# Second attention of a two-layer graph network: rough pair, scores, products in TensorE's step

## The reference

```
adj = jnp.maximum(adjacency_matrix, eye)
q, k, v = jnp.einsum('nd,hdk->hnk', node_matrix, Wqs), ...
scores = jnp.einsum('hqk,hmk->hqm', q, k) * kd ** (-0.5)
scores = scores + IDENTITY_BIAS * eye - MASK_VAL * (1.0 - adj)
att = jax.nn.softmax(scores, axis=-1)
return jnp.einsum('hqm,hmk,hko->qo', att, v, Wo)
```

## Time and profile before

| | |
|---|---|
| median of 3 runs | 4923.34 us (4919.93 to 4924.79) |
| the profiled execution's own time | 4912.91 us |
| its span | 4911.1 us |
| PE, DVE, ACT, POOL busy, share of the span | 84%, 74%, 74%, 7% |
| max passes (L1186) | 1024, mean 1224 ns |
| exponentials (L1149), seeds (L1135) | 1024 each, mean 1014 and 1028 ns |
| splits (L1211) | 1024, mean 693 ns |
| scores matmuls (L1081, L1086) | 2048 each, mean 381 and 380 ns |
| copies of `acc` (L1112) | 64, mean 800 ns |

### The profile page before, as it was taken

One profiled execution on the slowest core, in us unless ns is written; L12 is line 12 of the kernel. 1 busy time (PEld: TensorE's weight loads), 2 busy tenths in 40 slices (PEclk: granted clock), 3 DMA queues, 4 the chain that ended last, 5 costly groups with the idle time before them and its releaser, 6 DMA issues. The chain is left out here.

```text
span 4911.1 us, 106706 instructions
## 1 busy us (share of the span) xinstructions
PE 4141.8 (84%) x42500; PEld 2752.0 (56%) x42500; DVE 3639.4 (74%) x6026; ACT 3633.0 (74%) x4642; POOL 343.8 (7%) x527
## 2 busy tenths in 40 slices
PE   7922239889988999699929999999999999999977
PEld 4412228888888888544405555555555555555543
DVE  2245559999999999722238888888888888888834
ACT  1133349999999999511119999999999999999952
POOL 0000000000000000000020211111020202111000
PEclk9955559999999999899959999999999999999999
DMA  1299994544454445445463544545453635445223
GB/s 64 87 303 365 361 342 146 168 161 153 146 166 166 154 139 168 111 144 161 122 168 78 139 119 126 135 105 144 101 155 94 167 86 138 120 122 135 69 74 144
DMA packets 413633, 742.27 MB, mean 151 GB/s; under 512 B 90041, under 2 KB 282745, under 8 KB 376185
## 3 DMA queue, kind: packets, MB, share of 16 engines
q1 hardware_dynamic: 349296, 643.60, 43.5%
q0 software_dynamic: 20608, 75.51, 4.6%
q10 hardware_dynamic: 43280, 16.92, 1.3%
HBM read 567.42 MB, written 168.49 MB: 150 GB/s over the span
## 5 line engine op out<-in xcount | busy, mean ns | idle before, releaser
L1186 DVE CUSTOM_DVE_ANT_0 m_junk<-m_rough,m_rows 128x1024 bf16<-128x1024 f32 x1024 | 1253.4, 1224 | 293.8 <-PE m_rough L1053 226.3
L671 PE MATMUL g_acc<-g_vals,g_pos 128*128 128x130 f16 (+1 forms) x8192 | 1199.0, 250 | 130.9 <-DVE g_neg L626 104.4
L552 ACT ACTIVATE g_step<-g_arow,g_steep 128x512 bf16<-128x512 f32 x2048 | 1258.3, 712 | 58.6 <-DVE g_neg L626 38.2
L1135 ACT ACTIVATE m_scores<-m_strip 128x1024 f32<-128x1024 bf16 x1024 | 1052.9, 1028 | 103.3 <-POOL m_strip L984 39.3
L1149 ACT ACTIVATE m_whole<-m_scores 128x1024 int32<-128x1024 f32 x1024 | 1038.0, 1014 | 34.5 <-PE m_scores L1086 23.6
L1067 PE MATMUL m_acc<-m_v,m_halves 128*128 128x129 f16 (+1 forms) x16384 | 896.8, 208 | 45.3 <-ACT m_got L1112 45.3
L671 PEld LDWEIGHTS g_acc<-g_vals,g_pos 128*128 128x128 bf16 x8192 | 810.7, 99 | 208.5 <-DVE g_neg L626 106.5
L1067 PEld LDWEIGHTS m_acc<-m_v,m_halves 128*128 128x128 f16 x16384 | 750.7, 98 | 280.0 <-issue 185.9
L1081 PE MATMUL m_scores<-m_qA,m_kA 128*128 128x512 f16 x2048 | 780.5, 381 | 5.5 <-ACT m_scores L1135 5.4
L1086 PE MATMUL m_scores<-m_qB,m_kB 65*128 65x512 f16 x2048 | 779.2, 380 | 0.0
L624 DVE TENSOR_TENSOR g_pos<-g_step,g_strip 128x1024 bf16<-128x1024 bf16 x1024 | 679.9, 686 | 87.5 <-ACT g_step L552 65.7
(11 more groups left out here) (146 smaller groups left out, 3158.6 us busy)
## 6 DMA issues: line engine op xcount, KB each, us to landing
g_vals<-scr_gat_v SPq DMA_DIRECT2D x128, 1040.0 KB, 5.3
m_v<-scr_v SPq DMA_DIRECT2D x64, 1032.0 KB, 7.6
b_stage<-in_adj SPq DMA_DIRECT2D x64, 1024.0 KB, 9.8
m_kA<-scr_k_hi SPq DMA_DIRECT2D x128, 512.0 KB, 6.2
scr_row_mask<-b_rowm SPq DMA_DIRECT2D x64, 512.0 KB, 8.8
scr_no_edge_T<-b_colm SPq DMA_DIRECT2D x64, 512.0 KB, 8.3
g_strip<-scr_no_edge_T SPq DMA_DIRECT2D x64, 512.0 KB, 6.8
m_kB<-scr_k_lo SPq DMA_DIRECT2D x64, 512.0 KB, 5.4
```

What stands on the lines that cost most here:

```text
L552: ins = nc.scalar.activation(step[:, j % RING, t, :], arow[:, b, :], ACT.Sigmoid, scale=STEEP, bias=steep[:, b, 2 * j + t:2 * j + t + 1])
L671: mm = pe.matmul(acc[:, b, it, lo:hi], edges, vals[:, b, 2 * j + t, lo:hi], start=j == 0 and t == 0 and lo == 0, stop=j == PAIRS - 1 and t ...
L1135: nc.scalar.activation(scores[:, n % 2], strip[:, 2 * st:2 * st + 2, :].rearrange("p t i -> p (t i)"), ACT.Copy, scale=-BIG / 2).then_inc( ...
L1186: nc.vector.tensor_tensor_reduce(out=junk[:, n % 2], in0=rough[:].rearrange("p a m -> p (a m)"), in1=rows[:, n % TC, n // TC * WIDE:(n // ...
```

## The change

In TensorE's stream alone, the rough pair now stands ahead of the scores of its step, and no longer between scores and products:

```diff
             for g in range(U * STEPS):
-                score(g // STEPS, g // STEPS % SLOTS, g % STEPS)
                 if g + EARLY < U * TILES:
                     max_tile(g + EARLY)
+                score(g // STEPS, g // STEPS % SLOTS, g % STEPS)
                 if g >= LAG:
                     products((g - LAG) // STEPS, (g - LAG) // STEPS % SLOTS, (g - LAG) % STEPS)
```

## The result

The changed kernel takes 5089.46 us (median of 4 runs, 5088.25 to 5094.13) against 4922.35 us (4 runs, 4919.93 to 4924.79): ratio 1.0341, 95% interval 1.0323 to 1.0359, 167 us slower.

What follows compares the result with a forecast made beforehand. A closed chain of waits across ScalarE, VectorE and TensorE, 4.49 us over two steps, becomes the bound: 37.11 us per unit against 33.72, 62.25 x 3.39 = 211 us, plus 2 at the start, gives 5136 us, range 5090 to 5175.

Steps and rivals of the forecast that it cites:

- The chain: Exponential, split, max pass, rough pair, scores, exponential: 4.49 us over two steps, 2.245 per step; before, 5.19 over three.
- split start to max pass start: VectorE link from a split's start to the next max pass's start, put at 0.74 us.
- The other links: Exponential to split 1.04, max pass to rough pair 1.29, rough pair to scores 0.34, scores to exponential 1.08 us.
- The extras: Copy, reduction, division and small matmuls, work done once per unit that lengthens single steps.
- The division: VectorE, round 8: makes split to max pass 1.15 us, adding 0.41, felt by step 9.
- The reduction: VectorE, round 4, over the maxima: makes split to max pass 0.98 us, adding 0.24, felt by step 5.
- Products to rough pair: TensorE behind the copy: 0.70 us, within 5.14 from the exponential of step 2 to that of step 4.
- the odd chain: Odd steps from step 3 at 2.77 through seven links of 4.49; decides the unit's 37.11 us, the even steps giving 36.79.
- The step of TensorE: Cost of the rough pair's new neighbours on TensorE: put at nothing, bounded at 0.1 us per step either way.
- Extras are swallowed: Rival: copy, reduction and division hide in slack between even and odd steps; 36.14 us per unit, 5076 us; 7%.
- The clock: Granted clock stays 1.00; rival: TensorE's falls behind each unit's copy, 5248 us, 3%; harsher form near 6000, 1%.
- The own range: Range of the main forecast alone, 5105 to 5165 us, counting 0.03 us in each chain link as 15 us.

Runs made afterwards that it cites:

- rps: Kernel before, with the order rough pair, products, scores on TensorE, the rough pair ahead of its step's scores: 5582.82 us, ratio 1.1358.
- rsp_maxfirst: Changed kernel with VectorE's max pass ahead of the split in each round: 4941.94 us, ratio 1.0053 to the kernel before.
- rsp_maxfirst_copyearly: Changed kernel with VectorE's max pass ahead of the split and ScalarE's copy of acc ahead of the seed: 4875.44 us, ratio 0.9918 to the kernel before.
- rsp_divlate: Changed kernel with VectorE's division behind the max pass of its round instead of ahead of it: 5065.32 us, ratio 1.0307 to the kernel before.
- rsp_copyearly: Changed kernel with ScalarE's copy of acc ahead of the seed in step 2 of a unit: 5068.74 us, ratio 1.0312 to the kernel before.

## Why the prediction was right, and 47 us too high

**The chain.** Right, and shown by three kernels that differ in its length or its span: `rps` with the neighbours of before, 5.07 us over two steps (5.08 measured); the changed kernel, 4.37 over two; `rsp_maxfirst` with the neighbours of the changed kernel, the same links over three (hidden).

**The mis-sized term: split start to max pass start, 0.74.** This was a misreading of the earlier trace rows. The max pass at 2572.88 did not follow the split at 2572.14 as fast as it could; it was released by the rough pair that started at 2572.28, 0.60 us earlier. VectorE's own distance stood elsewhere in the trace before, in an operation behind a split that waits for nobody:

```profile
3561.66 0.69 DVE L1211 TENSOR_SCALAR m_halves<-m_whole 128x2048 f16<-128x2048 uint16 x1
3562.26 0.17 DVE L1202 RECIPROCAL m_rden<-m_den 128x4 f32<-128x4 f32 x1
```

That is 0.60, and the changed kernel has 0.61. The other links are together 0.01 longer than forecast, so a turn is 0.12 shorter, 4.37 for 4.49. It enters the forecast's unit seven times: 7 x 0.12 = 0.84 us per unit, 52 us in all, a little more than the whole error.

**The extras**, which took the 0.74 as their base, were wrong with it. The division adds 1.15 - 0.61 = 0.54 and not 0.41: 0.13 per unit back. The reduction adds 0.08 and not 0.24 (split at 3574.88, max pass at 3575.57), and is not on the path: step 5 comes 2.08 after step 4, by ScalarE. Step 5 thus stands 7.32 us behind step 2, where the forecast has 7.50. Products to rough pair take 0.80 (3574.07 to 3574.87) where I had put 0.70, so step 4 comes at 5.24 and not 5.14:

```profile
3574.07 0.86 PE L1067 MATMUL m_acc<-m_v,m_halves 128*128 128x129 f16 x16 [0.71 <-ACT m_got L1112]
3574.87 0.41 PE L1053 MATMUL m_rough<-m_kA,m_qC 64*128 64x512 f16 x2
3575.21 0.39 PE L1081 MATMUL m_scores<-m_qA,m_kA 128*128 128x512 f16 x1
```

With these the unit in view is 5.24 + 2.08 + 6 x 4.37 + 0.53 + 0.22 + 2.03 = 36.32 us, as its copies show (3573.13 to 3609.45). Against 37.11 that is 0.79 less: six links of 0.12 behind step 5, 0.18 up to it, and the 0.13 of the division the other way, to within rounding. That the odd chain carries the division and decides, and that step 18 follows it by ScalarE's pace, was right; between steps 2 and 5 the way led over the copy and step 4 instead.

**The step of TensorE.** Put at no cost, bounded at 0.1 us: it is 0.34 (rough pair to scores) + 0.88 (to products) + 0.80 (to rough pair) = 2.02, the same as before, and `rsp_maxfirst_copyearly` shows that it is worth nothing.

**The rival with the nearer number.** "Extras are swallowed" said 5076 us and 36.14 per unit, nearer to what was measured than my 5136 and 37.11. That is luck of its number: it holds the same 0.74. With the measured links it gives 8 x 4.37 + 0.22 = 35.18 per unit, and 36.39 was measured. `rsp_divlate` and `rsp_copyearly` show as well that division and copy are not hidden.

**The clock.** 1.00 in the stage as forecast, but for its very start: up to 2591 us it is at 0.50, and the first four steps take 2.6 to 3.0 us each, where the kernel before is at full clock from 2571 us on. That is part of the 9 us named above. The rival was met by accident in `rps`. The rule of the Trainium skill, page "TensorE: Matmul & The Clock Gate", section "A second HAM failure mode: psum-queue depth-cycling", on short pauses between groups of matmuls did not show in the changed kernel, with TensorE waiting in about every second step at a granted clock of 1.00.

**The own range** of the forecast, 5105 to 5165, was too narrow: 0.03 us per link is less than what a wrong reading of one link costs. The wider one, 5090 to 5175, reached down that far only for the swallowed case.

## What to carry to other kernels

For an instruction that is moved past another on its engine, write down every closed chain through it, its length and the number of steps it spans: 4.37 us over three steps was hidden, over two the kernel was 3.4% slower, and with 0.70 more (and a falling clock) 13.6%. Take each link where its receiver waits for that very releaser; a start-to-start distance is a link only if no other arrival stands just ahead of it. Where a chain binds, moving the other engine's operation by one place in its round (the max pass ahead of the split) can undo the loss as well as undoing the change.

## What I had not expected of the hardware

In `rps`, TensorE's products and scores ran at 1.2 GHz behind waits of 1.69 us, often enough to bring the granted clock of 3000 to 3300 to 0.96, but at 2.4 GHz behind waits of 2.13 us. In the changed kernel waits of 0.71 us once per unit left it at 1.00. So the length of the wait alone did not tell the clock behind it. And on VectorE the operation behind a split starts 0.08 to 0.09 us before the split's recorded end (a split of 0.69 us, the next start 0.60 to 0.61 after its own), so the sum of recorded durations is not the shortest distance between two of them.
